# A fused attention and quantised feed-forward layer on one core: a redone opening, and the second value product, the row maxima and the last weighing in another order

## What is computed

```python
# attention, 16 heads of 32
h = layernorm(x)
Q, K, V = split(h @ Wq.T + bq), split(h @ Wk.T + bk), split(h @ Wv.T + bv)
scores = Q @ K.T / sqrt(32)                    # causal, and minus (i - j) for key j < i
attn = softmax(scores)
x = x + layernorm((attn @ V) @ Wo.T + bo)
# feed forward
xh = layernorm(x) @ H                          # H: orthonormal 512 x 512 Hadamard matrix
xq = 4-bit levels of xh, one scale per row     # round(xh / s) * s
wq = ternary(weight)                           # -1, 0, 1 times the row's mean of |w|
x = x + layernorm(xq @ wq.T)
```

## Time and profile before

| what | us |
|---|---|
| three runs | 1225.76, 1227.17 (median), 1227.83 |
| profiled execution, its own time | 1227.52 |
| profiled execution, its span | 1226.0 |
| TensorE busy | 1096.9 (89%) |
| VectorE busy | 1003.5 (82%) |
| ScalarE busy | 704.3 (57%) |
| GpSimd busy | 597.3 (49%) |

### The profile page before, as it was taken

The page is one execution under the profiler, slowest core; times in us unless marked ns, Lnnn a source line. Parts: engine busy times, 40 slices in busy tenths (PEclk is TensorE's granted clock), DMA queues, the critical chain, the costliest instruction groups (busy, mean ns, idle before and its releaser), DMA issues.

```text
span 1226.0 us, 44860 instructions
## 1 busy us (share of the span) xinstructions
PE 1096.9 (89%) x18625; PEld 740.6 (60%) x18656; DVE 1003.5 (82%) x2552; ACT 704.3 (57%) x1491; POOL 597.3 (49%) x716
## 2 busy tenths in 40 slices
PE   1799999999999999999999999999999999999641
PEld 1466666666666666666666666666666666666320
DVE  2576888888888889888888899888888898887772
ACT  2544666566666665566666655666666655665431
POOL 0124455554555554545555555545555545445421
PEclk9889999999999999999999999999999999999765
DMA  5754665666656656665565657666575656554330
GB/s 176 183 123 105 138 132 139 145 121 144 148 135 141 144 133 143 123 139 147 139 146 138 137 133 156 120 139 150 136 150 134 135 141 135 128 132 106 61 69 36
DMA packets 206752, 161.82 MB, mean 132 GB/s; under 512 B 152368, under 2 KB 152624, under 8 KB 206448
## 3 DMA queue, kind: packets, MB, share of 16 engines
q1 hardware_dynamic: 201856, 141.86, 53.8%
q0 software_dynamic: 4688, 17.04, 3.8%
HBM read 40.87 MB, written 16.78 MB: 47 GB/s over the span
## 4 chain that ended last, share of the span: by engine, by line
PE 41%; DVE 27%; issue 11%; POOL 9%; ACT 9%; DMA 1%; SPq 1%; POOLq 0%; DVEq 0%; ACTq 0%
PE f_job L1185 29%; DVE f_bst L900 5%; POOL f_z L455 3%; PE f_st L1282 3%; POOL f_square L449 3%; DVE f_z L978 3%; PE f_o L1302 2%; PE f_o L1307 2%; POOL f_OTl L440 2%; DVE f_o L890 2%; DVE f_inverse L892 2%; DVE f_x L924 2%; DVE f_folded_x L941 2%; DVE f_y L932 2%; DVE f_y L931 1%
## 5 line engine op out<-in xcount | busy, mean ns | idle before, releaser
L434 POOL TENSOR_SCALAR_AFFINE_SELECT f_PT<-f_PT 64x512 f32<-64x512 f32 (+1 forms) x256 | 203.2, 818 | 68.5 <-ACT f_PT L578 44.7
L449 POOL TENSOR_TENSOR f_square<-f_stage 128x512 bf16<-128x512 f16 x128 | 130.3, 1040 | 155.2 <-ACT f_stage L556 154.9
L556 ACT ACTIVATE f_stage<-f_job,f_bias 128x256 f16<-128x256 f32 x256 | 106.2, 466 | 107.1 <-PE f_job L1185 95.2
L1185 PE MATMUL f_job<-f_xTh,f_wqh 128*128 128x256 f16 x512 | 140.4, 274 | 27.1 <-DVE f_wkl L755 24.5
L440 POOL TENSOR_TENSOR f_OTl<-f_o,f_OTh 128x256 f16<-128x256 f32 x128 | 86.4, 676 | 118.7 <-ACT f_OTh L596 118.1
L1185 PE MATMUL f_job<-f_xTl,f_wqh 128*128 128x256 f16 x512 | 140.2, 274 | 0.9 <-issue 0.9
L1185 PE MATMUL f_job<-f_xTl,f_wkh 128*128 128x256 f16 x512 | 140.0, 273 | 0.5 <-issue 0.5
L1185 PE MATMUL f_job<-f_xTh,f_wql 128*128 128x256 f16 x512 | 140.1, 274 | 0.0
L1185 PE MATMUL f_job<-f_xTh,f_wkl 128*128 128x256 f16 x512 | 140.0, 273 | 0.0
L1185 PE MATMUL f_job<-f_xTh,f_wkh 128*128 128x256 f16 x512 | 140.0, 273 | 0.0
L854 DVE SCALAR_TENSOR_TENSOR f_stage<-f_job,f_bias,f_stage 128x256 f16<-128x256 f32 x256 | 109.7, 477 | 35.9 <-ACT f_stage L556 35.8
(11 more groups left out here) (160 smaller groups left out, 2990.9 us busy)
## 6 DMA issues: line engine op xcount, KB each, us to landing
f_stacks<-f_stage SPq DMA_DIRECT2D x384, 128.0 KB
f_xin<-x SPq DMA_DIRECT2D x32, 512.0 KB, 4.9
f_x<-x SPq DMA_DIRECT2D x32, 512.0 KB, 4.2
out<-f_z POOLq DMA_DIRECT2D x32, 512.0 KB, 3.4
f_Vmix<-f_V SPq DMA_DIRECT2D x32, 256.0 KB
f_Vmix<-f_V SPq DMA_DIRECT2D x64, 128.0 KB
f_stacks<-rows_const SPq DMA_DIRECT2D x3, 512.0 KB, 7.1
f_stacks<-wqT SPq DMA_DIRECT2D x1, 1024.0 KB, 9.2
```

The lines of the kernel that those rows point to most:

```text
L434: nc.gpsimd.affine_select(out=d, in_=d, compare_op=ALU.is_ge, fill=0.0, base=odd * SUB, pattern=[[0, 4], [0, TP], [1, SUB]], channel_multi ...
L449: nc.gpsimd.tensor_tensor(square[:, 2 * m + pair, :], h, h, ALU.mult).then_inc(squared, 1)
L556: nc.scalar.activation(stage[:, 2 * m, g, :], bank("qk", g)[:, m * W2:(m + 1) * W2], ACT.Identity, bias=bias[:, m, g:g + 1]).then_inc(qk_h ...
L1185: mm = pe.matmul(dst, lhs[a](c), rhs[b](c), start=(n == 0), stop=(n == 3 * KC - 1))
```

## The change

In words, opening first:

- unit 0's power -0.5 is no longer GpSimd's: ScalarE takes the logarithm and the exponential of -0.5 times it (`first_root`), VectorE corrects it by one Newton step (`refine_root`). VectorE also normalises the second half of unit 0's block (`first_norm`). GpSimd's first power is now that of unit 1;
- the q and k weights are loaded, and their parts made, in halves; the first `qk` needs only the q halves to begin. The four bias vectors come as one small table made on the host;
- the transposing DMA of the high part no longer waits for the low part;
- TensorE's opening is a list of its own: `qk(0, ·)`, both value products of unit 0, `qk(1, 0)` and `qk(1, 1)`, the scores of unit 0 (now in the `st` and `o` banks), `qk(1, 2)`, `norms(0)`, `qk(1, 3)`, `turn_max(0)`, and only then the bias product (`fold_values`), the spread of the ternary scales and the turn of the ternary weights. VectorE's and ScalarE's lists follow it. Turn -1 is gone, and turn 0 begins at `keys(0, 0, 0)`;
- `weight_guard(s)` reads one matrix in each of the turns 0 to 3.

In every turn:

- `values(n, 1)` moves from before `keys(s, 3, ·)` to behind `scores(n, 0)`, `scores(n, 1)` and `norms(n)`, ahead of `weigh(s, 2)`;
- `weigh(s, 3)` moves from the end of turn s to behind `qk(·, 0)` of the next turn, with `invert` and `normalise` of that group;
- `ORDER` has `v1` behind `norms`. The banks follow: `scores(n, 0)` and `scores(n, 2)` now share bank 2, `scores(n, 1)` and `scores(n, 3)` bank 3, `values(n, 1)` is in bank 1 and `norms` in bank 0;
- VectorE takes `maxima(n, 0)`, `maxima(n, 1)` and then `keep_norms`, where it had one, `keep_norms`, and the other three later.

```diff
-         ("q", 0), ("y", 1), ("q", 1), ("f", 0), ("v", 0), ("f", 1), ("v", 1), ("s", 0),
-         ("norms", 0), ("s", 1), ("s", 2), ("s", 3))
+         ("q", 0), ("y", 1), ("q", 1), ("f", 0), ("v", 0), ("f", 1), ("s", 0), ("s", 1),
+         ("norms", 0), ("v", 1), ("s", 2), ("s", 3))
+HOMES = {("bv", 0): ("q", 0), ("ffscale", 0): ("q", 1), ("tern", 0): ("y", 0), ("tern", 1): ("y", 1)}
...
+        def score_bank(n, i):
+
+            return bank("s", i) if n else (ps_st + ps_o)[i]
...  SyncE: the order of the loads
-                sp.wait_ge(xl_made, m + 1)
                 until(sp, v_product, TP * (m - 1))
                 for half, src in enumerate((xh, xl)):
+                    sp.wait_ge((xh_made, xl_made)[half], m + 1)
...
             load_front(0)
+            load_qk_half(0, wqT, 0)
+            load_qk_half(0, wqT, 1)
+            load_qk_half(1, wkT, 0)
+            load_qk_half(1, wkT, 1)
+            sp.dma_start(bias[:], bias_cols).then_inc(bias_in, 16)
+            turn_x(0)
+            load_front(1)
+            load_vo(0, wvT)
+            load_vo(1, woT)
             sp.dma_start(ident, identity).then_inc(ident_in, 16)
...  GpSimd
-            front_root(0)
+            front_root(1)
...  ScalarE
+            def first_root():
+
+                act.wait_ge(f_veps_made, 1)
+                nc.scalar.activation(f_rstd, f_veps, ACT.Ln).then_inc(first_log, 1)
+                act.wait_ge(first_log, 1)
+                nc.scalar.activation(f_rstd, f_rstd, ACT.Exp, scale=-0.5).then_inc(first_guess, 1)
...
+            first_root()
+            front_norm(0, 0)
+            front_high(0)
+            qk_weights_high(0, 0)
+            qk_weights_high(0, 1)
+            qk_weights_high(1, 0)
+            qk_weights_high(1, 1)
+            qk_high_part(0, 0)
+            front_norm(1, 0)
+            front_norm(1, 1)
+            qk_high_part(0, 1)
+            vo_weights_high(0)
+            front_high(1)
+            qk_high_part(0, 2)
+            qk_high_part(0, 3)
             act.wait_ge(ident_in, 16)
             nc.scalar.activation(identb[:], ident, ACT.Copy).then_inc(identb_made, 1)
+            vo_weights_high(1)
+            sum_ff()
+            keep_v(0, 0)
+            keep_v(0, 1)
...  in turn 0, ahead of its exponentials
+                if s == 0:
+                    keep_max(0)
+                    keep_ffscale()
+                    keep_tern()
...  VectorE
+            def refine_root():
+
+                dve.wait_ge(first_guess, 1)
+                nc.vector.tensor_tensor(f_off, f_rstd, f_rstd, ALU.mult).then_inc(first_step, 1)
+                dve.wait_ge(first_step, 1)
+                nc.vector.scalar_tensor_tensor(f_off, f_off, -0.5, f_veps, ALU.mult, ALU.mult).then_inc(first_step, 1)
+                dve.wait_ge(first_step, 2)
+                nc.vector.scalar_tensor_tensor(f_rstd, f_off, 1.5, f_rstd, ALU.add, ALU.mult).then_inc(f_rstd_made, 1)
...
             front_stats(0)
+            refine_root()
             front_offset(0)
+            first_norm(1)
             front_low(0)
...
+            front_stats(1)
+            qk_low_part(0, 0)
+            front_offset(1)
+            qk_low_part(0, 1)
+            vo_weights_low(0)
+            front_low(1)
+            qk_low_part(0, 2)
+            qk_low_part(0, 3)
+            vo_weights_low(1)
+            spread_bv()
+            ternary()
+            maxima(0, 0)
...
+                if s < 4:
+                    weight_guard(s)
...
-                    normalise(s, 1)
-                if has(n):
-                    maxima(n, 0)
-                    keep_norms(n)
+                normalise(s, 1)
+                maxima(n, 0)
+                maxima(n, 1)
+                keep_norms(n)
...  TensorE
-                if has(n):
-                    values(n, 1)
-                if has(s):
-                    keys(s, 3, 0)
-                    keys(s, 3, 1)
-                if s == -1:
-                    turn_tern()
-                if has(n):
-                    scores(n, 0)
-                    norms(n)
-                    scores(n, 1)
-                if has(s):
-                    weigh(s, 2)
-                if has(n):
-                    scores(n, 2)
-                    scores(n, 3)
-                if has(s):
-                    weigh(s, 3)
+                keys(s, 3, 0)
+                keys(s, 3, 1)
+                scores(n, 0)
+                scores(n, 1)
+                norms(n)
+                values(n, 1)
+                weigh(s, 2)
+                scores(n, 2)
+                scores(n, 3)
```

404 lines of the change are left out of this document (211 added, 193 removed).

## The result

| | median, us | runs |
|---|---|---|
| before | 1226.58 | 1223.84 to 1227.83 (5) |
| changed | 1216.83 | 1215.36 to 1218.38 (5) |

The ratio is 0.9921, interval 0.9906 to 0.9936. The forecast was 1235.0 with a range of 1222 to 1244; the time lies under it.

A forecast was written before the change was run, and what follows sets the result against it. No engine alone bounds the kernel: each turn is VectorE up to the first maxima, then TensorE, in series. 1227.5 − 12 (opening) + 2 (guards) + 17 (28 turns) + 0.5 (last turn) = 1235.0 us, range 1222 to 1244.

The forecast's parts named there:

- D and the three waits: Turns: D, VectorE's first maxima's end, 14.08 us after y_out(k, 1) starts; scores(n, 2), scores(n, 3), qk at D + 0.05, 0.59, 1.19.
- "From there TensorE works on to the next out product", "together some 34.4": Steady turn: 14.08 us of VectorE up to D, then about 20.3 us of TensorE, in series.
- "`weigh(s, 3)`... its move costs nothing by itself": Turns: weighing of the last group moved behind the next qk(·, 0), same work on the same stretch, 0 us.
- +17 for the value product with the banks and the maxima: Turns: 28 x 0.70 = 19.6 us more TensorE time after D, less 3 of stalls swallowed; bounds +8 and +24.
- −12 for the opening, case A: Opening: GpSimd's first power costs 8.0 us when called, unit 1's out at 28.4, first exponential at 63.7; chance 0.52.
- rival B: Opening: GpSimd's start delay runs from program start, over by 14.50; opening −17.5, total 1229.5 us; chance 0.17.
- +2 for the guards: Turns 0 to 3: one 2.27 us guard read each exceeds VectorE's 1.36 us slack, late by about 0.9 to 1.1.
- The signs: Trace: wrong if turns keep 34.4 or less, TensorE's waits for maxima shrink, or the first exponential comes after 70.
- Rival C: Turns: the value product fills TensorE's 20.2 us wait for maxima, total 1197.3 us; chance 0.15 with its half-way case.
- Rival E: Turns: order does not bound them, no loss per turn, only the opening counts, 1217.5 us; counted within C's 0.15.
- the half-way case of C: Turns: the value product fills part of the wait, turns cost nothing net, 1217.5 us; within C's 0.15.

The follow-up runs named there:

- weigh_only: opening_only with only weigh(s, 3), invert and normalise of that group moved behind the next qk(·, 0); 1206.42 us, ratio 0.9847.
- opening_only: The kernel before with the changed opening and spread guards, old order in every turn; 1211.51 us, ratio 0.9875.
- finish_late: opening_only with GpSimd's finish_out (last addition and output DMA) moved behind the next front_root; 1220.01 us, ratio 0.9938.
- values_guards: Changed kernel with values(n, 1) and its banks back ahead of keys(s, 3), all four guard reductions in turn 0 where VectorE waits; 1202.89 us, ratio 0.9819.
- maxima_early: values_guards with maxima(n, 0) and maxima(n, 1) ahead of normalise(s, 1) from turn 1 on; 1201.44 us, ratio 0.9792.

## Why the prediction was wrong, step by step

- **D and the three waits** (right): `qk` at D + 1.18 for a forecast of 1.19, VectorE unbroken for 14.07 us, `scores(n, 2)` and `scores(n, 3)` at D + 0.05 and + 0.58.
- **"From there TensorE works on to the next out product", "together some 34.4"** (the step that failed in the turns). The 20.3 us after D were not all TensorE's work. In the turn shown `qk` began at D + 1.5, and the 18.8 us behind it hold 18.45 of TensorE's work (the least over the 27 turns) and waits for ScalarE of 0.2 to 0.5 us. A second closed path of about the same length runs through VectorE, ScalarE and GpSimd, and it held the turn in the kernel before. So some 0.4 of the 0.70 us that the new order adds to TensorE's way were free, and the turns grew by 0.35.
- **"`weigh(s, 3)`... its move costs nothing by itself"** (wrong). Forecast 0, measured −5.1 (weigh_only): the inversion leaves the place ahead of `heads_high(s, 1)` and `finish_out`, the power is 0.30 us early instead of 0.03, and TensorE has work where it waited.
- **+17 for the value product with the banks and the maxima** (right in sign and mechanism, too large): +10.4, weigh_only to the changed kernel. `qk` goes from D + 0.66 to D + 1.19, 27 x 0.53 = 14.3. The 3.9 between this and 10.4 may be stalls that vanish under the waits (8.0, 1.8 and 0.8 us of "issue" in weigh_only's waits, none in the changed kernel's); the prediction took 3 for these, and no run separates them.
- **−12 for the opening, case A** (the step that failed in the opening). `y_out(0, 1)` in opening_only is 18.3 us earlier; rival B said 17.5. The 8.0 us between input and power were read as the price of the first call. They were what was left of a delay that had begun at 2.44, when the power came to the head of the queue. The row had said so: 12.06 us of "issue" began before the input was there.
- **+2 for the guards** (right): 2.6.
- **The signs** that it named: TensorE's waits for maxima shrank (20.2 to 11.1 us), one of its signs of being wrong, as the wait moved in front of `values(n, 1)`, where it was said to be hidden. TensorE's first matmul came at 14.3 (forecast 16.5), and the first exponential at 55.6 (63.7 by A, 58 by B).
- **Rival C** (wait filled, 1197) did not occur: TensorE's idle time of the loop stayed, 35 us for 38. **Rival E** and the half-way case of C gave 1217.5, and 1216.8 was measured, but that is luck: they have turns that cost nothing and an opening of 10, and the runs show 5.3 lost in the turns and 15.1 gained in the opening.

The terms by runs: −15.1 (opening with guards), −5.1 (weighing), +10.4 (value product, banks, maxima); the forecast had −10, 0 and +17. They are differences along one row of kernels, so that their sum, −9.8, must come near the −9.7 measured and proves nothing; and another row has another split, since the order costs 7.4 behind the old opening.

In the changed kernel, half of what VectorE's list takes over finish_late's (26.76 for 26.10) is again the held statistic (0.51 for 0.17). Open: the other half, and how much each other part of the opening (halves of the weights, the earlier transposing DMA) brings; they weren't run alone. The two fastest kernels are values_guards with 1202.9 and maxima_early with 1201.4, 1.8 and 2.1% under the kernel before.

## What to carry to other kernels

Where engines take turns, look for every closed path of a turn, not only the one with the visible wait: a chain that gives 9% each to two engines that "have time" (GpSimd 49% busy, ScalarE 57%) names a second path, and it sets what a shortened first one is worth. Look at the weight loads' waits as well as the matmuls'; many small ones are a path that touches. And when a transfer has to land, put work there that is needed later; when a step is put beside another engine's long instruction, check what small instruction of the other path it meets.
